# Three batches' last comparison tiles moved from VectorE to GpSimd, with new instruction orders on all engines

## What is computed

```python
x = x + attn(_layernorm(x))       # q, k = elu(.)+1, k normalised per head; scores @ v; Wo; layernorm * gamma + beta
h = _layernorm(x)
k = max(1, int(L * 0.75))
scores = jnp.einsum('bld,d->bl', h, w_router)
_, top_idx = jax.lax.top_k(scores, k)
processed = gelu(take(h, top_idx) @ w_block)
out = h.at[batch_idx, top_idx].set(processed)
x = x + out
```

## Time and profile before

| | |
|---|---|
| median of 3 runs | 91.2 us (91.19 to 91.83) |
| profiled execution, its own time | 91.51 us |
| its span, first to last instruction | 89.8 us |
| granted TensorE clock, mean | 0.992 of full |
| instructions | 2397 |

### The profile page before, as it was taken

How to read it: one execution, slowest core, us unless ns; L and a number is a source line. 1 busy time by engine, 2 the same in 40 slices (tenths; PEclk the granted TensorE clock), 3 DMA queues, 4 the chain that set the end, 5 groups by cost and what they waited for, 6 DMA issues and landing times.

```text
span 89.8 us, 2397 instructions
## 1 busy us (share of the span) xinstructions
PE 79.9 (89%) x816; PEld 68.4 (76%) x816; DVE 80.9 (90%) x258; ACT 66.9 (75%) x186; POOL 52.8 (59%) x79
## 2 busy tenths in 40 slices
PE   4998689999999999999999599999999797999700
PEld 1335656976797997999999599999998797779600
DVE  4368999999797897999999999999999999999960
ACT  5003599998999996753539799999799696998700
POOL 5265885989992997659770979769838400000000
PEclk9999999999999999999999999999999999999996
DMA  0899969970999999900000000000000000348456
GB/s 24 233 256 319 280 168 319 290 189 7 143 127 140 139 143 136 112 10 0 0 0 0 0 7 0 0 4 7 0 4 0 0 7 10 107 121 236 138 149 180
DMA packets 18113, 8.99 MB, mean 100 GB/s; under 512 B 819, under 2 KB 18102, under 8 KB 18102
## 3 DMA queue, kind: packets, MB, share of 16 engines
q1 hardware_dynamic: 13232, 6.49, 26.7%
q0 software_dynamic: 4160, 2.10, 21.5%
q10 hardware_dynamic: 710, 0.26, 1.1%
HBM read 4.66 MB, written 2.10 MB: 75 GB/s over the span
## 4 chain that ended last, share of the span: by engine, by line
PE 46%; DVE 41%; issue 4%; ACT 3%; DVEq 1%; POOL 1%; ACTq 0%
DVE beats L918 11%; PE bank L1219 7%; PE bank L1211 7%; PE bank L1152 6%; DVE xb_sb L886 5%; DVE x_sb L941 5%; DVE bn L893 4%; PE bank L1252 4%; PE bank L1228 4%; PE bank L1253 4%; PE bank L1188 3%; PE bank L1271 3%; DVE beats L927 2%; DVE bn L818 2%; DVE x_sb L853 2%
## 5 line engine op out<-in xcount | busy, mean ns | idle before, releaser
L918 DVE TENSOR_SCALAR beats<-s_row,s_col 128x1024 bf16<-128x1024 f32 (+7 forms) x32 | 15.5, 541 | 0.0
L595 ACT ACTIVATE norm_sb<-xb_sb,shift,gain 128x128 f32<-128x128 f32 x32 | 13.2, 507 | 2.7 <-DVE shift L847 2.7
L1252 PE MATMUL bank<-M_sb,qT 128*128 128x128 f32 x64 | 12.5, 277 | 0.0
L1253 PE MATMUL bank<-back,hT 128*128 128x128 f32 x64 | 12.4, 275 | 0.0
L413 POOL TENSOR_TENSOR r<-var,minus_half 128x4 f32<-128x4 f32 x8 | 8.1, 1025 | 5.8 <-DVE var L833 5.5
L400 POOL TENSOR_TENSOR k_sb<-k_sb,k_rnorm 128x512 f32<-128x512 f32 x8 | 9.3, 1252 | 2.7 <-DVE k_rnorm L801 2.7
L426 POOL TENSOR_TENSOR r<-var,minus_half 128x4 f32<-128x4 f32 x8 | 9.1, 1194 | 2.9 <-DVE var L839 2.9
L1252 PEld LDWEIGHTS bank<-M_sb,qT 128*128 128x128 f32 x64 | 9.7, 192 | 0.2 <-ACT M_sb L558 0.2
L1253 PEld LDWEIGHTS bank<-back,hT 128*128 128x128 f32 x64 | 9.7, 192 | 0.0
L588 ACT ACTIVATE x_sb<-bank,r 128x128 f32<-128x128 f32 x32 | 9.2, 383 | 0.2 <-DVE s_col L901 0.2
L1219 PEld LDWEIGHTS bank<-w_c,hT 128*128 128x128 f32 x56 | 6.9, 192 | 2.1 <-ACT hT L513 1.1
(11 more groups left out here) (132 smaller groups left out, 216.7 us busy)
## 6 DMA issues: line engine op xcount, KB each, us to landing
xb_sb<-in_L_attn_x_dram SPq DMA_DIRECT2D x4, 512.0 KB, 6.8
xb_sb<-beta_sb POOLq DMA_DIRECT2D x4, 512.0 KB, 8.4
x_sb<-in_L_attn_x_dram SPq DMA_DIRECT2D x7, 256.0 KB, 5.2
out_dram<-x_sb SPq DMA_DIRECT2D x7, 256.0 KB, 2.3
x_sb<-in_L_attn_x_dram SPq DMA_DIRECT2D x2, 128.0 KB, 2.7
out_dram<-x_sb SPq DMA_DIRECT2D x1, 128.0 KB, 2.4
out_dram<-x_sb ACTq DMA_DIRECT2D x1, 128.0 KB, 2.5
w_sb<-in_L_attn_Wq_dram ACTq DMA_DIRECT2D x1, 64.0 KB, 2.5
```

Of the source, the lines that this page charges most:

```text
L595: last = nc.scalar.activation(norm_sb[:, t], xb_sb[:, t], ACT.Identity, bias=shift3[:, t:t + 1], scale=gain3[:, t:t + 1])
L918: nc.vector.tensor_scalar(beats[:, b % 2, J, P * J:T * P], s_row[:, b, P * J:T * P], s_J, None, ALU.is_le).then_inc(beats_done, 1)
L1252: nc.tensor.matmul(o, qT[:, u, t * P:(t + 1) * P], M_sb[:, b], start=True, stop=False)
L1253: last = nc.tensor.matmul(o, hT[:, u, t * P:(t + 1) * P], back[:], start=False, stop=True)
```

## The change

Tiles 6 and 7 of batches 0, 1 and 2 are compared on POOL, which signals them through a semaphore of its own, beats_pool. mask_own of the second half waits for both counts; `compared` counts only DVE's tiles. masks, on POOL, comes behind scale_k(1) and three add_beta. All engine lists and the table of banks are new; every other operation is the same and on the same engine.

```diff
+    POOL_TILES = (2, 2, 2, 0)
...
         def compared(b, J):
-            return T * b + TILE_ORDER[b].index(J) + 1
+            return sum(T - n for n in POOL_TILES[:b]) + TILE_ORDER[b].index(J) + 1
+
+        def half_compared(b, half):
+            return compared(b, min(TH * half + TH, T - POOL_TILES[b]) - 1)
...
+            def compare(b, J, part):
+
+                s_J = s_col[:, T * b + J:T * b + J + 1]
+                pool.wait_ge(s_row_done, 2 * b + 2)
+                if b >= 2 and J == T - POOL_TILES[b]:
+                    pool.wait_ge(first_full, b - 1)
+                    pool.wait_ge(last_full, b - 1)
+                nc.gpsimd.tensor_scalar(beats[:, b % 2, J, P * J:T * P], s_row[:, b, P * J:T * P], s_J, None,
+                                        ALU.is_le).then_inc(beats_pool, 1)
...
             def mask_own(b, half):
...
-                dve.wait_ge(beats_done, compared(b, TH * half + TH - 1))
+                dve.wait_ge(beats_done, half_compared(b, half))
+                if half and POOL_TILES[b]:
+                    dve.wait_ge(beats_pool, sum(POOL_TILES[:b + 1]))
...
             def row_sums(b, half):
                 if b == 0:
                     pe.wait_ge(mask_set, 1)
-                pe.wait_ge(beats_done, compared(b, TH * half + TH - 1))
+                pe.wait_ge(beats_done, half_compared(b, half))
...
-            masks()
             add_beta(0)
+            add_beta(1)
+            add_beta(2)
             scale_k(0)
             scale_k(1)
-            add_beta(1)
-            add_beta(2)
+            masks()
+            add_beta(3)
             scale_k(2)
...
-            compare(0, 6, 1)
-            compare(0, 7, 1)
```

More of the change, by code:

```diff
@@ L405, in mask_own @@
                     pool.wait_ge(mask_set, 1)
-                pool.wait_ge(beats_done, compared(b, TH * half + TH - 1))
+                pool.wait_ge(beats_done, half_compared(b, half))
+                if half and POOL_TILES[b]:
+                    pool.wait_ge(beats_pool, sum(POOL_TILES[:b + 1]))
                 o = own_blocks(b, half)
@@ L441, in _ @@
             roots1(4)
-            masks()
             add_beta(0)
+            add_beta(1)
+            add_beta(2)
             scale_k(0)
             scale_k(1)
-            add_beta(1)
-            add_beta(2)
+            masks()
+            add_beta(3)
             scale_k(2)
             scale_k(3)
-            add_beta(3)
             scale_k(4)
+            scale_k(5)
             roots2(0)
-            scale_k(5)
+            residual(0)
             roots2(1)
-            residual(0)
+            roots3(0)
             scale_k(6)
+            roots2(2)
+            roots3(1)
+            roots2(3)
+            roots3(2)
             scale_k(7)
[L458 to L461, removed]
             roots2(4)
@@ L465, in _ @@
             gelu_sum(1)
-            roots3(2)
             roots3(3)
+            compare(0, 6, 1)
             roots3(4)
+            compare(0, 7, 1)
             roots2(6)
@@ L675, in _ @@
             gelu(1, 0)
+            copy_xT(3)
+            gelu(1, 1)
             copy_hk(3)
             copy_s_row(0)
-            gelu(1, 1)
-            copy_xT(2)
             copy_s_row(1)
@@ L975, in _ @@
             bn_x(7)
+            k_half(1)
+            key_sums(0)
             normalise1(4)
-            k_half(1)
-            normalise1(5)
-            key_sums(0)
+            shifts1(4)
             key_sums(1)
             q_half(0)
+            q_half(1)
+            normalise1(5)
             normalise1(6)
-            shifts1(4)
             k_half(2)
+            k_half(3)
             key_norms(0)
-            k_half(3)
-            q_half(1)
             k_half(4)
-            q_half(2)
@@ L990, in _ @@
-            q_half(3)
+            k_half(5)
             key_sums(2)
             key_sums(3)
-            k_half(5)
+            q_half(2)
             centre_wo()
+            q_half(3)
+            q_half(4)
+            key_norms(1)
             mask_vk(0)
-            key_norms(1)
             key_sums(4)
             key_sums(5)
-            q_half(4)
             k_half(6)
+            k_half(7)
             key_norms(2)
-            k_half(7)
-            key_sums(6)
-            variances2(0)
@@ L1005, in _ @@
             q_half(5)
             q_half(6)
+            variances2(0)
+            key_sums(6)
+            key_sums(7)
+            scale_y(0)
             mask_vk(1)
-            scale_y(0)
+            q_half(7)
+            y_gamma(1)
             variances2(1)
-            y_gamma(1)
-            key_sums(7)
-            q_half(7)
+            x1_stats(0)
+            mask_vk(2)
+            variances3(0)
+            key_norms(3)
             residual(1)
-            key_norms(3)
-            x1_stats(0)
+            affine3(0)
@@ L1016, in _ @@
             x1_stats(1)
-            mask_vk(2)
             variances2(2)
             y_gamma(2)
+            variances3(1)
             y_stats(3)
-            variances3(0)
-            variances3(1)
+            residual(2)
             variances2(3)
[L1024 to L1028, removed]
             y_stats(4)
             x1_stats(2)
-            x1_stats(3)
+            y_gamma(3)
+            variances3(2)
@@ L1032, in _ @@
             y_stats(5)
-            score_cols(0, 1)
+            affine3(1)
+            residual(3)
             variances2(4)
             variances2(5)
+            score_cols(0, 0)
+            score_cols(0, 1)
+            y_gamma(4)
             score_cols(1, 0)
+            y_gamma(5)
             score_cols(1, 1)
-            variances3(2)
-            y_gamma(4)
-            y_gamma(5)
             residual(4)
+            affine3(2)
+            x1_stats(3)
+            x1_stats(4)
+            mask_vk(3)
@@ L1042, in _ @@
             residual(5)
-            affine3(1)
-            mask_vk(3)
-            x1_stats(4)
-            x1_stats(5)
             variances3(3)
@@ L1051, in _ @@
             compare(0, 2, 1)
-            affine3(2)
+            score_cols(2, 0)
+            score_cols(2, 1)
+            x1_stats(5)
+            y_stats(6)
             compare(0, 3, 1)
@@ L1117, in _ @@
             compare(3, 7, 1)
-            merge(1)
-            merge(2)
+            gelu_sum(6)
             compare(3, 0, 1)
             compare(3, 1, 1)
+            mask_own(3, 1)
             merge(3)
-            drop_first(2)
             compare(3, 2, 1)
             compare(3, 3, 1)
+            drop_first(2)
+            mask_own(3, 0)
             drop_last(2)
-            affine3(7)
-            mask_own(3, 1)
             merge(4)
-            mask_own(3, 0)
             merge(5)
-            gelu_sum(6)
             gelu_sum(7)
             drop_last(3)
+            merge(7)
             drop_first(3)
-            merge(7)
             merge(6)
```

215 lines of the change are left out of this document (107 added, 108 removed), and 23 rows, old and new, of the table BANK_USES.

## The result

The changed kernel takes 92.35 us (median of 6 runs, 91.86 to 93.0), the kernel before 91.36 in the same number of runs: ratio 1.011, interval 1.006 to 1.015. It is 1% slower, where 0.9% faster was forecast, and lies outside the range. In all that follows, ratios and intervals leave out executions over 1.5% longer than the fastest of their kernel, which ran at a lower granted clock. The profiled execution took 92.62 us with a span of 90.9 (before 91.51 and 89.8).

What follows compares the result with a forecast made beforehand. DVE was taken to set the pace from the middle on. From 91.5 us: -1.38 comparisons, 0 old stalls in new places, +0.4 port, +0.2 idle, -0.8 in all: 90.7, as a median 90.4; range 88.6 to 91.8.

Steps and rivals of the forecast that it cites:

- What bounds the kernel: From the middle on DVE sets the pace; an instruction taken from it behind 35 us is worth its pitch.
- -1.38 for the comparisons: Three pairs of comparisons leave DVE in batches 0 to 2, 0.46 us each: 1.38 us less.
- +0.4 for their port: The six comparisons on POOL hold DVE up through the shared port: 0 to 1.6 us, taken as 0.4.
- the cover of 4 to 5 us: POOL's comparisons end 4 to 5 us before mask_own wants them, so no term for waits.
- At six in ten that is 1.75, as much as before. I put the change at 0.: Old DVE stalls of 1.78 us against five possible new meetings of 2.9: change 0, ends -1.78 and +1.1.
- The walk: Each engine's new order followed with the pitches of the old rows, to find starts, waits and port meetings.
- PE loses nothing: Early part: attention_matrix(0) starts near 24.9 instead of 24.23, but q_proj(6), formerly behind it, now stands ahead.
- rival B: POOL's early queue runs late through add_beta issues, making DVE and PE wait: +1.3, so 92.5 us; chance 0.15.
- Rival C: POOL's comparisons hold DVE up by 1.4 us, or ACT or PE takes the end over: 91.4 us; chance 0.15.
- Rival A: New orders keep wide POOL work and DVE's fast form apart, 1.5 us of stalls go: 88.7 us; chance 0.22.
- The rule of the exclusive lock: Port shared by DVE and POOL: first to start holds it its whole instruction; three stalls agreed, the power didn't.
- the walk's two sums: Without stalls, DVE's first comparison of batch 0 stands at 53.4 and its last merge ends at 84.1.

Runs made afterwards that it cites:

- C: The kernel of experiment 2 with variances2(2) on DVE moved behind y_gamma(2), away from scale_k(7): 90.24 us, ratio 0.987 to the kernel before.
- experiment 2: The kernel before, its orders and banks kept, with the six comparisons alone moved to POOL: 90.93 us, ratio 0.994 to the kernel before.
- experiment 1: The changed kernel's new orders and banks with all comparisons back on DVE: 93.41 us, ratio 1.023 to the kernel before.
- Experiment 6: The changed kernel with POOL's early order of before, masks first, then one add_beta: 91.86 us, ratio 1.004 to the kernel before.
- Experiment 5: Three kernels: the kernel before plus four late POOL comparisons (92.01 us profiled), additions (97.86 us median) or powers (91.46 us median) beside seven DVE comparisons.
- experiment 3: The changed kernel with five small DVE steps moved out of four meetings with wide POOL work: 91.62 us, ratio 0.999 to the kernel before.
- B: The changed kernel with the repairs of experiment 3 and Experiment 6, and gelu_sum(4) on DVE ahead of gelu_sum(5): 91.01 us, ratio 0.994 to the kernel before.
- experiment 4: The kernel before with 15 extra POOL comparisons and multiplications of 128 to 1024 columns behind the last merge: 109.5 us in all.

## Why the prediction was wrong

**What bounds the kernel** was right: DVE ended last, more than before (63% of the chain), and an instruction taken from it or a stall removed moved the end by about its length (C against experiment 2: 0.59 of stall, 0.60 of timeline, 0.69 of median).

**-1.38 for the comparisons, +0.4 for their port.** Right within 0.2: together -0.98 was forecast, and -0.80 by the timelines or -1.06 by the medians came in the new orders (experiment 1 against the changed kernel), the port taking 0.57. In the old orders it took 0.84, and the -0.53 there contains 0.73 of an old stall. POOL's price for one was taken at half of the true one, and (2,7) ended at 76.17, not near 70, since (2,6) waited for its row of scores until 71.78. It did no harm, but the cover of 4 to 5 us was thinner than walked: the comparisons were done 1.6, 3.8 and 2.4 us ahead of the masks that want them. The prediction had said that one of over 1 us on POOL would make all of it wrong; the means were 1.09 and 1.31, and the end didn't notice.

**"At six in ten that is 1.75, as much as before. I put the change at 0."** This is the step that failed: the term of the sum for old stalls in new places was mis-sized. The walk had found five named places with a price each, 2.9 us; the sum took six tenths of it, for no reason in a row. All five came, 2.97 us, and a sixth of 0.53 that the walk missed because it had scale_k(4,5) end at 33.75 instead of 34.94. So the term put at 0 measured 2.97 + 0.53 - 1.78 = +1.72. With its own five prices the walk would have given 2.9 + 0.4 - 1.78 = +1.5 in all for the port, and the forecast 91.5 - 1.38 + 1.5 + 0.2 = 91.8, or 91.5 as a median. The high end of that term, +1.1, was in the prediction, but as an unlikely end. With the sixth stall, and 0.57 instead of 0.4 beside POOL's comparisons, the same sum gives 92.6, the profiled time.

**"PE loses nothing" in the early part.** Key norms came at 22.78, not 22.2, and attention_matrix(0) at 25.65, not 24.9. Experiment 6 puts this at 0.49 us by the medians. It was not POOL's queue that was late, as rival B had it: the three issues took 4.92 us, less than the 5.7 walked, and POOL then waited for DVE's key norms. DVE's normalise1 were slow beside them. Nobody waited for the masks. So rival B had the place and the sign, not the mechanism or the size; that its 92.5 lies nearest to the measured 92.35 is luck.

**Rival C**, that POOL's comparisons give back what they save, is out for the changed kernel, where they gave back 0.57 of 1.38 us. In the old orders, at 0.84 and a wait of 0.26, it was most of the truth. **Rival A** was the opposite of what came.

**The rule of the exclusive lock.** The rows of before said that wide POOL work holds DVE up and the power doesn't. Experiment 5 shows three degrees: 4.04 of 6.03 us for additions over 512 columns, 1.02 of 4.87 for comparisons over 256, 0 of 4.80 for powers over 4.
The Trainium skill, "SBUF — State Buffer", section Who interferes with whom, has the first to issue hold the shared ports for its whole instruction; the additions come near that, the comparisons and powers don't, and the measurement decides.
The same section of the Trainium skill says that a DVE instruction with two SBUF inputs contends with a GpSimd instruction that reads SBUF; the mask of 1.38 us instead of 0.41 in experiment 3 agrees.

**What stays open.** The orders still cost something when repaired: B, at 91.01, is 0.77 behind C. The wait of 0.65 for PE in the repaired orders, the 0.60 of gelu_sum(4) on DVE and the sixth stall (0.72 instead of 0.16 at 34.03 in B, which no repair moved) are in it; they weren't tried apart. Nor is it settled what part of an add_beta slows normalise1. And the walk's two sums close without the 0.87 us of normalise1, so the walk seems to have been slower than the kernel somewhere else by about as much; where is open.

## What to carry to other kernels

When a walk by measured durations lands on named collisions, put them into the sum at their full price; a discount needs a row of its own. Judge moved work and a new order separately, by what each does to the stalls: here, by the medians, the work gained 1.1 us and the order lost 2.0. Before giving GpSimd a wide two-input instruction, look at what VectorE does at that moment. In this kernel its residuals, which read PSUM, kept their pace there; tensor_scalar from SBUF to SBUF and two-operand masks didn't. Check after each repair, and after each gain, what slid into its place.

## What the runs showed of the hardware

- GpSimd instructions hold VectorE's fast comparisons up by very different shares of their time: two thirds for f32 additions over 512 columns (4.04 of 6.03 us), a fifth for comparisons with a per-row scalar over 256 (1.02 of 4.87), nothing for powers over 4 (0 of 4.80).
- The victims need not be wide: 4-column instructions of 0.16 us took up to 0.85 and ended with the GpSimd instruction beside them; so the price is that of the waiting, not of the work.
- A comparison costs GpSimd 2.5 ns per column (VectorE 0.52) and 0.29 us to begin with (experiment 4). Over 512 columns that is 1.56 us, more than the two-input multiplication's 1.25.
- A stall on VectorE can cost more than itself: 4.04 us of it cost 6.4, with TensorE idle for 4 us and then at a granted clock of 0.50 for six.
